# GAT scores from folded weights, a one-hot for the last expert, and the norm inside its neighbours

## The reference

```
layer 0: graph convolution with 20000 edges (src, dst sorted, weight), flow attention, ternary FFN
layer 1 FFN:   S = softmax(xn @ Wg)            # 8 experts
               per expert: the 156 rows with the largest S are gathered, gelu(. @ W1 + b1) @ W2 + b2,
               times S, added back to their rows
layer 2 GNN:   gat_conv twice, relu after each, then @ fcW + fcb
   gat_conv:   h = (x @ W) as 4 heads of 256
               a_src = sum(h * att_src), a_dst = sum(h * att_dst)     per node and head
               e = leaky_relu(a_src[src] + a_dst[dst], 0.2), softmax over the edges into dst (with self loops)
               out[dst] = sum of alpha * h[src]  + bias
layer 2 mix:   attention by positive random features, 8 heads, with its own Wq, Wk, Wv, Wo
layer 2 FFN:   16 experts chosen by a tree
```

## Time and profile before

| | us |
|---|---|
| median of 3 runs (2026.96 to 2034.44) | 2030.32 |
| the profiled execution | 2031.14 |
| its span, first to last instruction | 2029.4 |
| PE busy | 1691.4 (83%) |
| DVE, ACT, POOL busy | 794.5, 481.3, 108.7 |
| mean granted clock of TensorE | 0.911 |

### The profile page before, as it was taken

How to read it: one execution, slowest core, us unless ns; L and a number is a source line. 1 busy time by engine, 2 the same in 40 slices (tenths; PEclk the granted TensorE clock), 3 DMA queues, 4 the chain that set the end, 5 groups by cost and what they waited for, 6 DMA issues and landing times. The chain is left out here.

```text
span 2029.4 us, 26209 instructions
## 1 busy us (share of the span) xinstructions
PE 1691.4 (83%) x8924; PEld 1036.5 (51%) x8925; DVE 794.5 (39%) x2027; ACT 481.3 (24%) x941; POOL 108.7 (5%) x173
## 2 busy tenths in 40 slices
PE   6598989999998899916989996678768999979973
PEld 3245564575474799913666644536213333355542
DVE  6455377611334544414454236422101111241555
ACT  2011224410110122201563115300213322221120
POOL 0011000000000022230000000000000000110000
PEclk9688999999999799957999997796979999979996
DMA  4131135100200577541000201016796399150000
GB/s 142 42 106 46 41 119 210 41 0 1 109 1 28 185 234 246 167 150 51 31 21 0 114 0 73 1 76 259 315 429 262 136 410 429 50 159 0 0 1 25
DMA packets 66780, 238.97 MB, mean 118 GB/s; under 512 B 13597, under 2 KB 17364, under 8 KB 59283
## 3 DMA queue, kind: packets, MB, share of 16 engines
q1 hardware_dynamic: 51565, 210.17, 27.4%
q0 software_dynamic: 15136, 27.77, 4.5%
HBM read 230.44 MB, written 7.43 MB: 117 GB/s over the span
## 5 line engine op out<-in xcount | busy, mean ns | idle before, releaser
L101 PE MATMUL psum<-a_second 128*125 128x512 f32 (+1 forms) x320 | 129.1, 561 | 2.9 <-DVE a_second L2320 2.2
L101 PE MATMUL psum<-a_h,a_u 125*125 125x257 f32 x400 | 95.9, 403 | 36.2 <-DVE a_first L2267 23.4
L98 PE MATMUL psum<-1_ident,1_xn_rows 125*128 125x125 f32 x120 | 23.0, 373 | 107.8 <-PEq L353 79.1
L101 PEld LDWEIGHTS psum<-a_h,a_u 125*125 125x125 f32 x400 | 79.7, 201 | 51.7 <-DVE a_first L2267 24.7
L833 DVE TENSOR_SCALAR a0e_ring<-a0e_node,a0e_key 125x625 f16 x198 | 69.9, 390 | 84.2 <-PE psum L649 77.9
L101 PE MATMUL psum<-a_W,1_xn_turned 128*125 128x512 f32 x200 | 96.6, 635 | 0.0
L101 PEld LDWEIGHTS psum<-a_second 128*125 128x125 f32 x320 | 58.1, 194 | 66.7 <-issue 62.8
L647 PE MATMUL psum<-a0e_ring,a0e_tables 125*128 x198 | 70.5, 413 | 19.9 <-DVE a0e_ring L833 12.3
L2619 PE MATMUL psum<-e_Wa,e_xgT 128*32 128x256 f32 x960 | 80.1, 389 | 3.5 <-DMA e_Wa<-in_L_ffn_W 3.5
L101 PE MATMUL psum<-a_W,a0l_H 128*125 128x512 f32 x190 | 82.3, 594 | 0.7 <-issue 0.7
L2599 PE MATMUL psum<-e_Wa,e_xgT 128*32 128x256 f32 x960 | 62.2, 401 | 22.3 <-DVE e_xgT L2826 15.1
(11 more groups left out here) (611 smaller groups left out, 2964.3 us busy)
## 6 DMA issues: line engine op xcount, KB each, us to landing
e_Wa<-in_L_ffn_W SPq DMA_DIRECT2D x28, 2048.0 KB, 18.6
e_Wb<-in_L_ffn_W SPq DMA_DIRECT2D x28, 2048.0 KB, 20.2
e_W<-in_L_ffn_W SPq DMA_DIRECT2D x16, 2048.0 KB, 12.4
1_xn_turned<-half_shares SPq DMA_DIRECT2D x16, 256.0 KB, 8.2
a_second<-in_L_gnn_W SPq DMA_DIRECT2D x1, 4096.0 KB, 12.6
a_W<-in_L_gnn_W SPq DMA_DIRECT2D x3, 1024.0 KB, 5.1
a_qkv<-half_shares SPq DMA_DIRECT2D x11, 256.0 KB, 3.6
a_W<-in_L_ffn_w_down POOLq DMA_DIRECT2D x1, 2816.0 KB, 16.0
```

The costliest lines, as they stand in the source:

```text
L98: last = nc.tensor.transpose(bank[0:rows, at:at + cols], terms[0], terms[1])
L101: last = nc.tensor.matmul(bank[0:rows, at:at + cols], lhs, rhs, start=(n == 0), stop=(n == len(terms) - 1))
```

## The change

1. Layer 0: `load_step` reads one register at a time. PE reads five behind each of the projections q2 to q4 and k0 to k4; DVE reads 8 behind each of its four table passes and the last eight among the `key` passes.
2. Layer 1's attention: the store of `c.AT` to memory is issued at the end of its SP stream.
3. Layer 1's FFN: POOL adds the self loops to `c.CT`; PE and ACT make the masks into `c.AT`. The last expert's rows aren't written and gathered: its one-hot is turned (`turn_places`), and ten matmuls bring its rows to the nodes. Expert 6 is turned before hidden(7). DVE folds the attention vectors into the GAT weights (`fold_attention`, `ahead.wa`) for both GAT layers, with `L2_gnn_W1` kept in `ahead.W1` and `L2_gnn_W2` staged by rows. The norm for layer 2 runs in the same block.
4. Layer 2's attention is one block. The scores are matmuls of 8 columns with the folded weights (`scores`), all projections of a GAT layer come before its aggregations, the mix is spread between the heads of the first, `fcb` is added by POOL, half of the turning is copied by DVE, and the last head's tiles alternate with turning and the last product. `W2` comes in two halves. The norm for the FFN runs in the same block.
5. Layer 2's FFN: only the turning block is left of `norm_phases`, which is gone.

The diff, cut to its core:

```diff
+            def load_step(engine, steps, n):
+
+                ends, shifts = steps
+                k = n % WINDOWS
+                if n < WINDOWS:
+                    ends.append(engine.value_load(step_i[k:k + 1, 1:2], min_val=2 * (k + 1), max_val=EDGE_TILES * (k + 1)))
+                else:
+                    shifts.append(engine.value_load(step_i[k:k + 1, 0:1], min_val=-EDGE_TILES * WINDOWS,
+                                                    max_val=EDGE_TILES))
 
...
+                        if t >= 2:
+
+                            pe.wait_ge(sem["steps_known"], 1)
+                            for n in range(5 * (t - 2), 5 * (t - 1)):
+                                load_step(pe, steps, n)
...
                         project("k", t)
-                    pe.wait_ge(sem["steps_known"], 1)
-                    ends, shifts = load_steps(pe)
+                        for n in range(5 * (t + 3), 5 * (t + 4)):
+                            load_step(pe, steps, n)
+                    ends, shifts = steps
...
+                    steps = ([], [])
+                    dve.wait_ge(sem["steps_known"], 1)
+                    for n in range(8):
+                        load_step(dve, steps, n)
+                    dve.wait_ge(sem["targets_made"], 1)
                     for a in range(3):
                         last = nc.vector.tensor_tensor(table[:, :, 1 + a, :], table[:, :, 0, :],
                                                        piece[:, a, :].unsqueeze(2).to_broadcast([ROWS, EDGE_TILES, WIN]),
                                                        ALU.mult)
-                    dve.wait_ge(sem["steps_known"], 1)
-                    ends, shifts = load_steps(dve)
+                        for n in range(8 * (a + 1), 8 * (a + 2)):
+                            load_step(dve, steps, n)
                     for k in range(WINDOWS):
+                        if k % 2:
+                            n = 4 * 8 + k // 2
+                            if n < LOADS:
+                                load_step(dve, steps, n)
                         last = nc.vector.scalar_tensor_tensor(out=key[:, k, :], in0=col[:, 2, :], scalar=float(k),
                                                               in1=col[:, 0, :], op0=ALU.is_equal, op1=ALU.mult)
...
+                sync.dma_start(c.saved_AT, c.AT[:, :, :]).then_inc(sem["weights_saved"], 16)
+                sync.wait_ge(sem["weights_saved"], 16)
...
                         spread(e + 2)
                     if e + 1 < EXP1:
                         gather(e + 1)
+                    if e == last_expert:
+                        turn_places()
                     output(e)
+                    if e == last_expert - 1:
+                        turn(e)
                     if e + 1 < EXP1:
                         hidden(e + 1)
-                    turn(e)
+                    if e != last_expert - 1:
+                        turn(e)
+                kept(("turn", last_expert, 1))
+                for t in range(TILES):
+                    for_dve(("sum", t), [product(ROWS, [(PT[0:TOPC, i, rows_of(t)], rows[:, last_expert % 2, i, :])
+                                                        for i in range(2)], DIM)])
 
             @block.scalar
             def _(act):
...
+                def fold_attention(unit):
+
+                    k, layer2 = unit % CH, unit >= CH
+                    if unit == 0:
+                        dve.wait_ge(sem["gat_landed"], 16)
+                        dve.wait_ge(sem["att1_landed"], 32)
+                    if unit == CH:
+                        dve.wait_ge(sem["att2_landed"], 32)
+                    if layer2:
+                        dve.wait_ge(sem[f"stage_landed{unit % 2}"], 16 * ((unit - CH) // 2 + 1))
+                    weights = stage[:, unit % 2, :] if layer2 else ahead.W1[:, k, :]
+                    start = done.count
+                    for hd in range(GAT_HEADS):
+                        cols = slice(hd * GAT_HID, (hd + 1) * GAT_HID)
+                        for w in range(2):
+                            n = w * GAT_HEADS + hd
+                            nc.vector.tensor_tensor_reduce(
+                                out=junk[:, w, 0:GAT_HID], in0=weights[:, cols], in1=att[:, w, cols], scale=1.0, scalar=0.0,
+                                op0=ALU.mult, op1=ALU.add, accum_out=ahead.wa[:, unit, n:n + 1]).then_inc(done.sem, 1)
+                            if done.up() > start + 1:
+
+                                dve.wait_ge(done.sem, done.count - 1)
+                    dve.wait_ge(done.sem, done.count)
+                    nc.vector.engine_nop().then_inc(sem["att_folded"], 1)
+
                 nc.vector.memset(rank[:, :, :, :], 0.0)
...
-                combine(EXP1 - 1)
-                dve.wait_ge(sem["rows_added"], TILES * EXP1)
+                    if 1 <= e < last_expert:
+                        fold_attention(2 * e - 2)
+                        fold_attention(2 * e - 1)
+                dve.wait_ge(sem["rows_added"], TILES * last_expert)
+                for t in range(TILES):
+                    nc.vector.scalar_tensor_tensor(out=c.x[:, t, :], in0=take(("sum", t))[0:ROWS, :],
+                                                   scalar=gate[:, t, last_expert:EXP1], in1=c.x[:, t, :], op0=ALU.mult,
+                                                   op1=ALU.add).then_inc(sem["vector_freed"], 1)
+                    dve.wait_ge(sem["vector_freed"], for_vector.met)
+                    last = norm.take_stats(t)
+                    if t >= TILES - 2:
+                        norm.on_vector(dve, t - (TILES - 2), last)
+                dve.wait_ge(norm.rows_normed, TILES)
 
             @block.sync
...
+                    if e >= 4:
+
+                        sync.wait_ge(sem["att_folded"], 2 * e - 4)
+                        if e == 4:
+                            for w, name in enumerate(["src", "dst"]):
+                                sync.dma_start(att[:, w, :], bcast(d[f"L2_gnn_att_{name}2"], 128)).then_inc(
+                                    sem["att2_landed"], 16)
+                        for b in range(2):
+                            sync.dma_start(stage[:, b, :], w_view(d["L2_gnn_W2"])[:, 2 * (e - 4) + b, :]).then_inc(
+                                sem[f"stage_landed{b}"], 16)
...
+                def scores(L):
+                    xT, chunks = [(c.xnT, CH), (outT, 2 * CH)][L]
+                    for_dve(("a", L), [product(ROWS, [(xT[:, k, rows_of(t)], wa[:, CH * L + k, :]) for k in range(chunks)],
+                                               2 * NH, at=2 * NH * t) for t in range(TILES)])
...
+                for t in range(TILES):
+                    turn_out(0, t, 0, for_act)
+                    turn_out(0, t, 1, for_dve)
+                pe.wait_ge(sem["w20_landed"], 16)
+                kept(("turn", 0, 0, 0))
+                used(("turn", 0, 0, 1))
+                project(1, 0, 0)
+                kept(("turn", 0, TILES - 1, 0))
+                used(("turn", 0, TILES - 1, 1))
+                scores(1)
+                project(1, 0, 1)
                 sources(1, 0)
-                for t in range(1, TILES):
+                project(1, 0, 2)
+                project(1, 0, 3)
+                sources(1, 1)
+                shifts(1, 0)
+                project(1, 0, 4)
+                shifts(1, 1)
+                pe.wait_ge(sem["w21_landed"], 16)
+                for t in range(TILES):
                     project(1, 1, t)
-                shifts(1, 0)
-                shifts(1, 1)
-                sources(1, 1)
                 aggregate(1, 0)
                 shifts(1, 2)
                 aggregate(1, 1)
                 shifts(1, 3)
                 aggregate(1, 2)
+                for t in range(TILES):
+                    turn_out(1, t, 0, for_dve)
+                for t in range(TILES + 2):
+                    if t < TILES:
+                        total(1, 3, t)
+                    if 1 <= t <= TILES:
+                        turn_out(1, t - 1, 1, for_act)
+                    if t >= 2:
+                        joined(t - 2)
...
+                for t in range(TILES):
+                    turned_bank(1, t, 0)
+                for t in range(TILES + 2):
+                    if t < TILES:
+                        combine_tile(1, 3, t)
+                    if t >= 2:
+                        add_bank(t - 2, "fc")
+                        dve.wait_ge(sem["vector_freed"], for_vector.met)
+                        last = norm.take_stats(t - 2)
+                        if t >= TILES:
+                            norm.on_vector(dve, t - TILES, last)
+                dve.wait_ge(norm.rows_normed, TILES)
...
-            norm_phases(core, c, c.x, c.xn, c.xnT)
+            turn_phase(core, c, c.xn, c.xnT, CH)
...
```

664 lines of the change are left out of this document (333 added, 331 removed).

## The result

| | before | after |
|---|---|---|
| median of the runs measured together, us | 2028.64 | 1934.54 |
| the profiled execution | 2031.14 | 1930.76 |
| its span | 2029.4 | 1929.0 |
| PE busy | 1691.4 | 1716.5 |
| PE idle (span less busy) | 338.0 | 212.5 |

The account below looks back on a forecast made before the run. TensorE was taken as the engine to follow, its holes and slow clock as the gain: 17.8 + 40.0 + 41 + 7.7 = 106.5; 2031.1 - 106.5 - 0.8 = 1923.8, said as 1924 us. Range 1904 to 1947, the forecast's own 1911 to 1937.

Parts of the forecast that it names:

- Part 1: Layer 0: register loads spread behind projections and table passes hide there; gain 17.8 us, bounds 3 to 22.
- Part 2: End of layer 1's experts: last expert put back by one-hot matmuls, norm inside; gain 40.0 us, bounds 30 to 45.
- 9 us of slack, so its price is nothing: Layer 1's experts: VectorE's fold delays the choice for e+3 to 15.5, its gather needs it at 24.4; no cost.
- rival 3: Layer 1's experts: 8 MB more loads slow the row-return chain, choice and weights come late; slower, 2041 us; chance 0.03.
- signs of being wrong: Expert waits on `chosen` or weights, periods over 24, late `targets_made`, or banks waiting for ScalarE behind its exponents.
- Part 3: Inside layer 2's attention: 426.0 us falls to 385, with 14.5 us of stalls left; gain 41, bounds 20 to 52.
- warm I take 0.11 each, 4.4 + 8.8 = 13.2 for both: Layer 2's attention: 40 and 80 narrow score instructions run at the warm price, adding 13.2 us to TensorE.
- all 8.6 us of slow clock in the aggregations: Layer 2's attention: the 400 aggregation matmuls' 8.6 us slow-clock excess, tied to stalls, was subtracted from TensorE's work.
- Part 4: Hole before layer 2's experts: norm moved ahead of the load-issuing section, 18.6 becomes 10.9 us; gain 7.7, bounds 4 to 11.
- Loads that don't hide: Layer 0: each projection waits for the five loads behind the one ahead; part 1 gains 3, total 1939; chance 0.12.
- ScalarE and VectorE as the bound: Layer 2's attention: their new order limits it, exponents hold the bank ring; part 3 gains 20, total 1945; chance 0.12.
- A last expert that gains less: Layer 1's experts: the last expert or the norm gains less, the rest as forecast; total 1933; chance 0.08.

## Why the prediction was right or wrong

**Part 1, 21.8 instead of 17.8.** The step that failed: "the sequencer needs 8 x (3.3 + 0.8) = 32.7 us from about 27, so it is through at 59.5". It ran from 25.5 to 52.1. The loads took 26.6 us, nearly the 26.2 of the block; the 0.8 us for sending a projection off, eight times, which I had called an estimate, is 0.4 us in all. So five loads (3.3 us) fit behind each projection (3.43) without the sequencer falling back. The Trainium skill (Advanced Engine Details and Errata, "Engine Queue Depths") has a queue of 64, by which all loads hide, and they did. But the 7.9 us of lead in the earlier trace rows weren't put to the test: in the changed kernel the loads begin 6.3 us before the end of the projection that they stand behind (25.5; the zero matmul at 55.84 less seven projections of 3.43 is 31.8), and by their even pace the last five begin at 48.8, 7.0 us before the zero matmul. Whether the lead could be longer, no run shows.

**Part 2, 36.1 instead of 40.0.** The end came as worked out: the one-hot is worth 13.4, the hole is 8.1. Expert 6 was forecast to be turned at 849.8 + 0.9, 197.0 us after the stage's start; it was turned at +201.7, and its rows then took 21.4, as forecast (21.3). That delay is the whole shortfall: 2.76 us of wait at the turn of expert 5, 0.47 at that of expert 6, and some 1.7 of slow clock behind the first (1.63 and 6.62 for two rows that take 1.04 and 5.54 elsewhere). The step that failed: "9 us of slack, so its price is nothing". It was counted with rows that return in 21.3 us, the chain of the last expert; from a turn to the addition of its rows it was 26.9 among the experts even before (787.61 to 814.47, rows that I hadn't looked at), and for expert 3 it became 32.2 (765.76 to 797.97). And the slack was taken to the gather, whereas TensorE turns before it gathers and VectorE makes `e_oT` behind the choice: to that turn there were 7 us (15.5 + 1.2 against 23.7), and the turn is what waited. That is close to rival 3's mechanism, at its own threshold ("from 30 us of chain on the choice is late"), for one expert instead of six and at 3 us instead of 12. One of the prediction's signs of being wrong came true with it, a period over 24 (26.70). The cause wasn't mainly the added bytes of the staged loads, which I had priced (without them 4.5 of the 5.7 us stay), but most likely the wait of SP behind the folding, which I had held harmless since "some 30 us [are] left until it's needed". The weights were late for nobody, but they now met the gathers. With the folding first the stage is 234.8, a gain of 41.4.

**Part 3, 34.5 instead of 41.** The stalls: forecast 14.5, idle 12.4; the one before head 2 was forecast at 4.9 and is 4.90, the wait for `combine(1, 2)` at 5.0 and is 3.97. The 0.93 before it is the same kind of wait one head earlier, for `combine(1, 1)` behind `take_higher(1, 2)`, and wasn't forecast; banks held by ScalarE were given 2 and took 0.67. The step that failed is the work: "warm I take 0.11 each, 4.4 + 8.8 = 13.2 for both". They took 6.79 + 12.61 = 19.4, and the products behind them 6.43 and 9.95 where 3.6 and 7.0 are warm: 12.0 in all. The earlier trace rows held the hint, the same kind of matmul at 0.165 in layer 1, which I read as forty at the slow clock. They weren't. The granted clock of the kernel before in two parts of that very run (columns as in the earlier trace rows):

```profile
658.50:660.00 1.50, 1.50 (x14) 1.50 (x15) 0.00 (x0) 1.16 (x1) 0.00 (x0) 1.00 1.03 426
663.00:665.10 2.10, 2.10 (x11) 2.01 (x10) 0.00 (x0) 0.00 (x0) 0.00 (x0) 0.50 1.05 396
```

It began at 2.4 GHz with 0.11 us an instruction and ended at 1.2 GHz with about 0.2: the clock fell inside a run of narrow products there too, before any change, and 0.165 is the mean of both prices. I did not ask whether such a run could cool a warm engine. The other part of the error: I gave back all 8.6 us of slow clock in the aggregations, but two stalls were still forecast, and 94.2 - 4 x 21.83 = 6.9 stayed. The two make 18.9 against 379.1 - 370.2 = 8.9 found, so 10 us of other work came out cheaper than in my sum. Most of it is slow clock that the mix had behind its own stalls in the kernel before, and that I didn't give back. Two of its groups, before and then after:

```profile
L101 PE MATMUL psum<-1_xn_turned,a_second 128*128 128x312 f32 (+1 forms) x128 | 35.7, 440 | 3.9 <-ACT a_second L2117 3.9
L101 PE MATMUL psum<-a_second,a_both 128*128 128x313 f32 (+1 forms) x32 | 13.0, 494 | 5.2 <-ACT a_wide L2073 5.2
```

```profile
L101 PE MATMUL psum<-1_xn_turned,a_second 128*128 128x312 f32 (+1 forms) x128 | 34.0, 426 | 0.0
L101 PE MATMUL psum<-a_second,a_both 128*128 128x313 f32 (+1 forms) x32 | 11.0, 426 | 0.0
```

With `a_omk` (6.5 to 5.5) and `a_omq` (6.1 to 5.5) they are 5.3 us cheaper, and the forty instructions of 130 columns another 1.8 (2.05 + 5.04 against five times 1.05). The other 3 us are open.

**Part 4, 8.4 instead of 7.7.** The hole is 10.24 against 10.9.

**The rivals.** Loads that don't hide: fell. ScalarE and VectorE as the bound: fell, no projection waited more than 0.7 us for ScalarE. A last expert that gains less: true of the stage by 3.9, through another mechanism than its own. GpSimd's additions were free for the reason that VectorE stood still beside them (883.7 to 889.9, its next pass at 891.1), not because they cost nothing. In sum 1930.8 in the profiled execution against 1924.6 forecast for it; the median of four is 3.8 higher. Where that lies isn't shown, since the other three have no trace, but unchanged stretches vary by more. That the total came within 10 us is in part luck: parts 1 and 4 gained 4.7 more than forecast, parts 2 and 3 lost 10.4.

## What to carry over

A slack is to be worked out with the latest time at which its inputs have come, not with the usual one, and to the first deadline behind it; and a wait put on a queue of transfers moves bytes in time, which matters to whoever shares the rings even if the data itself is never late. Long runs of matmuls with few columns belong between wide ones. "First all of this, then all of that" gives away the work that could have covered the chains between the parts: find the longest chain that repeats (here 18.2 us from shift to weights) and put as much other work between its start and its use.

## What was not expected of the hardware

- Forty products (eighty instructions) of eight columns in one run took the clock of a fully busy TensorE from 2.4 to 1.2 GHz, 13.7 us long; spread among wide ones they cost 0.11 to 0.13 us an instruction and the clock stayed up. That is worth 5.0 us in the second GAT layer, and in the first, where a gap stands before them, 2.6 between two executions. The kernel before has the same fall in its own run of forty.
- Register loads of TensorE (0.66 us each) ran 26.6 us at an even pace behind projections that were issued ahead, and hid wholly; in a block they idle the array for 18.35 us.
- GpSimd's additions and VectorE's two-input passes nearly exclude each other: 8.0 became 13.0 us, and 1.26 became 1.83.
- Unchanged stretches of 572 and 655 us vary by up to 9 and 12 us between kernels, whereas the stretch of the attention from the turns of `a_a` to those of the mix's keys takes 138.63 or 138.64 us in all kernels that leave it alone, but for the run with GpSimd's additions moved.
